# First half of the context finished inside the last group of heads, two unread matmuls in the first steps, copies ahead of the magnitudes

## What is computed

```python
q, k, v = x @ w_q.T, x @ w_k.T, x @ w_v.T           # 16 heads of 16
scores = where(mask, rope(q) @ rope(k).T * SCALE, -inf)
ctx = softmax(scores) @ v
x = layernorm(x + ctx @ w_o.T)
h = silu(x @ w_gate) * (x @ w_up)
h_sparse = the two largest magnitudes of every four
x = layernorm(x + h_sparse @ w_down)
```

## Time and profile before

| | us |
|---|---|
| median of 3 runs | 1748.93 (1747.69 to 1752.15) |
| profiled execution | 1751.17 |
| its span | 1749.4 |
| PE busy | 1486.2 (85%) |
| DVE busy | 1140.8 (65%) |
| ACT busy | 732.8 (42%) |
| POOL busy | 244.8 (14%) |
| granted clock of PE, mean | 0.914 of 2.4 GHz |

### The profile page before, as it was taken

One profiled execution on the slowest core, in us unless ns is written; L12 is line 12 of the kernel. 1 busy time (PEld: TensorE's weight loads), 2 busy tenths in 40 slices (PEclk: granted clock), 3 DMA queues, 4 the chain that ended last, 5 costly groups with the idle time before them and its releaser, 6 DMA issues.

```text
span 1749.4 us, 25732 instructions
## 1 busy us (share of the span) xinstructions
PE 1486.2 (85%) x9682; PEld 827.5 (47%) x9683; DVE 1140.8 (65%) x2275; ACT 732.8 (42%) x1232; POOL 244.8 (14%) x249
## 2 busy tenths in 40 slices
PE   4999999877989983589878988878998788988796
PEld 2666666653657873223343533253533254433355
DVE  5666666636421135678669779768779678688475
ACT  5444455512212220426744137843137752157530
POOL 3344444411410001000020000120000120000000
PEclk8999999978999977758999979998979998989999
DMA  2000001005105512222101022101022101221000
GB/s 111 13 25 25 24 26 33 24 13 180 36 24 148 157 38 105 42 37 43 31 16 34 1 43 55 37 19 31 6 38 56 43 19 25 37 34 34 31 1 25
DMA packets 137483, 75.21 MB, mean 43 GB/s; under 512 B 117648, under 2 KB 126352, under 8 KB 136592
## 3 DMA queue, kind: packets, MB, share of 16 engines
q1 hardware_dynamic: 136800, 72.02, 16.6%
q0 software_dynamic: 576, 1.77, 0.4%
HBM read 37.59 MB, written 9.06 MB: 27 GB/s over the span
## 4 chain that ended last, share of the span: by engine, by line
issue 58%; POOL 3%; DVE 0%; POOLq 0%; DVEq 0%
POOL xs_sb L1448 1%; POOL rs_sb L1442 1%; POOL ve_sb L1439 0%; POOL qks_sb L1462 0%; POOL v_sb L1460 0%; DVE bn_sb L1620 0%; POOL qks_sb L1452 0%; DVE x_sb_sb L1635 0%; POOLq L1159 0%; POOLq L66 0%; DVE mv_sb L1626 0%; DVEq L1159 0%; POOL v_sb L1459 0%; POOL qks_sb L1463 0%; DVE ident_h_sb L1808 0%
## 5 line engine op out<-in xcount | busy, mean ns | idle before, releaser
L1522 ACT ACTIVATE room_sb<-s_ps 128x1024 f32<-128x1024 f32 (+1 forms) x320 | 291.2, 941 | 173.7 <-PE s_ps L1965 169.8
L1686 DVE TENSOR_REDUCE mx_sb<-s_ps 128x1 f32<-128x512 f32 (+1 forms) x400 | 249.6, 650 | 73.1 <-PE s_ps L1941 46.8
L1938 PE MATMUL s_ps<-room_sb 48*128 48x512 f16 (+3 forms) x480 | 155.9, 362 | 30.2 <-DVE mx_sb L1681 17.1
L1985 PE MATMUL cm_ps<-room_sb,v_sb 128*32 128x512 f32 (+3 forms) x1536 | 171.3, 536 | 0.8 <-ACT room_sb L1528 0.8
L1965 PE MATMUL s_ps<-room_sb 51*128 51x128 f16 (+4 forms) x1152 | 154.1, 288 | 15.4 <-ACT room_sb L1522 10.6
L2080 PE MATMUL cm_ps<-w_fd_sb,room_sb 128*128 128x256 f32 x512 | 132.7, 408 | 13.3 <-DVE room_sb L1764 13.3
L1439 POOL TENSOR_TENSOR ve_sb<-mv_sb,eps_sb 128x4 f32<-128x4 f32 x24 | 5.0, 210 | 951.2 <-DVE mv_sb L1626 951.2
L396 DVE SCALAR_TENSOR_TENSOR x_sb_sb<-xp_sb,conv_w_sb,x_sb_sb 128x512 f32<-128x512 f32 x96 | 106.7, 1114 | 22.6 <-ACT x_sb_sb L319 20.5
L1938 PEld LDWEIGHTS s_ps<-room_sb 48*128 48x128 f16 x480 | 42.9, 96 | 165.3 <-DVE mx_sb L1686 84.4
L2080 PEld LDWEIGHTS cm_ps<-w_fd_sb,room_sb 128*128 128x128 f32 x512 | 98.3, 200 | 38.1 <-issue 14.1
L2067 PE MATMUL s_ps<-xbT_sb,w_fg_sb 128*128 128x512 f16 x384 | 103.3, 400 | 14.3 <-DVE ctok_sb L1734 12.7
(11 more groups left out here) (256 smaller groups left out, 2942.7 us busy)
## 6 DMA issues: line engine op xcount, KB each, us to landing
we_gu_sb<-we_gu SPq DMA_DIRECT2D x32, 352.0 KB
we_dn_sb<-we_dn SPq DMA_DIRECT2D x32, 176.0 KB
x_in_sb<-x SPq DMA_DIRECT2D x9, 512.0 KB, 3.6
rows<-x_sb_sb SPq DMA_DIRECT2D x8, 512.0 KB, 3.0
x_sb_sb<-rows SPq DMA_DIRECT2D x2, 2048.0 KB, 11.4
out<-x_sb_sb SPq DMA_DIRECT2D x8, 512.0 KB, 2.6
room_sb<-qks_sb SPq DMA_TRANSPOSE x88, 3.3
xp_sb<-w_in SPq DMA_DIRECT2D x1, 1024.0 KB, 5.6
```

The source lines that it names most:

```text
L1522: act.activation(weights[(g * NU + u) % SLOTS_P][:, 2 * pair:2 * pair + 2, 0:width(u) * P], W[s % 2][:, :, 0:width(u) * P], ACT.Exp, scale ...
L1686: dve.tensor_reduce(mx[:, pair, k % 2, slot:slot + 1], max_bank(g, m)[:, 0:count * P], AX.X, ALU.max, negate=True).then_inc(mx_ok, 1)
L1938: last = pe.matmul(bank[:, at * P:(at + plain) * P], query[head:head + NORM, i * P:(i + 1) * P], key[head:head + NORM, j * P:(j + plain) * ...
L1985: last = pe.matmul(O[32 * h:32 * h + 32, (i - half * GT) * P:(i - half * GT + count) * P], v[:, j, g * HG + h, :], weights[(g * NU + u) % ...
```

## The change

In the last group the first half of the context is transposed (steps 10 and 11), copied by DVE, projected (a tile in each of steps 13 to 16), added to x and normalised; its transposes for the hidden layer stand right behind the last weighted sums, ahead of the last sums' transposes, in the two halves of bank S[2]. Behind the heads only the second half of the context is transposed. Its projection stands on PE behind the first hidden chunk, ahead of the second tile's `qkv`. In each of the first eight steps of a sequence two unread 128x512 matmuls go ahead of the scores. In the rotation loop ACT copies the next tile ahead of the magnitude. The LayerNorms of the next x move to the end of the third group and the start of the fourth, "f" of a first half into the hidden layer of its own sequence (chunks 13 and 14), "f" of a second half to steps 3 and 6. `mv` and `rs` have two buffers each. The diff, cut to its core:

```diff
@@ -1251,12 +1251,12 @@
...
         for b in range(NB):
-            if b > 0:
-                ORDER += [("f", b - 1, 0), ("f", b - 1, 1)]
...
                 ORDER += [("x", b + 1, 0), ("x", b + 1, 1)]
-            ORDER += [("a", b, 0), ("a", b, 1)]
-        ORDER += [("f", NB - 1, 0), ("f", NB - 1, 1)]
+            if b > 0:
+                ORDER.append(("f", b - 1, 1))
+            ORDER += [("a", b, 0), ("a", b, 1), ("f", b, 0)]
+        ORDER.append(("f", NB - 1, 1))
...
@@ -1346,6 +1346,10 @@
...
             return S[0] if c == 0 and t % 2 else S[2]
+
+        def half_banks(s):
+
+            return (C, M) if s else (S[2][:, 0, :], S[2][:, 1, :])
...
@@ -1465,10 +1469,10 @@
...
                 kind, b, s = ORDER[k]
+                if (kind, s) == ("a", 0) and b + 1 < NB:
+                    x_low(b + 1, 0)
+                    x_low(b + 1, 1)
...
-                if (kind, s) == ("x", 1):
-                    x_low(b, 0)
-                    x_low(b, 1)
...
@@ -1537,13 +1541,13 @@
...
                             sums_copied(b, g, 0)
-                        if g == NHG - 1 and b + 1 < NB and s >= STEPS - 2:
-                            x_high(b + 1, s - STEPS + 2)
+                        if g == NHG - 1 and b + 1 < NB and s in (8, 9):
+                            x_high(b + 1, s - 8)
...
             def high_chunks(b, s):
-                wait(act, wo_mm, 2 * b + 2)
-                for f, bank in enumerate((C, M)):
+                wait(act, wo_mm, 3 * b + 2 + s)
+                for f, bank in enumerate(half_banks(s)):
...
@@ -1582,13 +1586,12 @@
...
                 heads(b)
-                wait(act, tc, 2 * b + 2)
-                act.activation(xbT[:, 1, :].rearrange("p (a c) -> p a c", a=2), S[1][:, :, :], ACT.Copy).then_inc(cTa_ok, 1)
+                high_chunks(b, 0)
+                wait(act, tc, 3 * b + 3)
+                act.activation(xbT[:, 1, 1, :], M, ACT.Copy).then_inc(cTa_ok, 1)
...
                     qkv_copied(c, 0)
-                high_chunks(b, 0)
-                if ahead:
...
@@ -1600,12 +1603,12 @@
...
                         part_copies(c, w + 1)
+                    if ahead and w + 2 < ST:
+                        qkv_copied(c, w + 2)
...
                         magnitude(b, w)
-                    if ahead and w + 2 < ST:
-                        qkv_copied(c, w + 2)
...
@@ -1620,10 +1623,28 @@
...
                 wait(dve, bn_ok, k + 1)
-                wait(dve, ln_ok, k)
+                wait(dve, ln_ok, k - 1)
...
                 for t in range(GT):
-                    last = dve.bn_aggr(mv[:, t, :], bn[:, t, :])
+                    last = dve.bn_aggr(mv[:, k % 2, t, :], bn[:, t, :])
+                last.then_inc(mv_ok, 1)
+
+            def first_stats(b):
+                k = LN["a", b, 0]
+                wait(dve, mv_ok, k)
+                for t in range(GT):
+                    if t % 2 == 0:
+                        wait(dve, wo_mm, 3 * b + t // 2 + 1)
+                        own = x_sb[:, b * ST + t:b * ST + t + 2, :]
+                        dve.tensor_tensor(own, S[2][:, t // 2, :].rearrange("p (t c) -> p t c", t=2), own, ALU.add).then_inc(xr_ok, 1)
+                        wait(dve, xr_ok, 3 * b + t // 2 + 1)
+                    last = dve.bn_stats(bn[:, t, :], x_tile(b, t))
+                last.then_inc(bn_ok, 1)
+                wait(dve, bn_ok, k + 1)
+                wait(dve, ln_ok, k - 1)
+                dve.sem_inc(passed, 1)
+                for t in range(GT):
+                    last = dve.bn_aggr(mv[:, k % 2, t, :], bn[:, t, :])
...
@@ -1795,11 +1815,22 @@
...
                                 maxima(b, of, low, high)
-                        if g == NHG - 1:
-                            if b > 0 and s in (2, 6):
-                                finish(b - 1, s // 4)
-                            if b + 1 < NB and s in (10, 14):
-                                layernorm("x", b + 1, s // 4 - 2)
+                        if b + 1 < NB and (g, s) == (NHG - 2, 16):
+                            stats("x", b + 1, 0)
+                        if b + 1 < NB and (g, s) == (NHG - 2, 18):
+                            stats("x", b + 1, 1)
+                            normal("x", b + 1, 0)
+                        if b + 1 < NB and (g, s) == (NHG - 1, 0):
+                            normal("x", b + 1, 1)
+                        if b > 0 and (g, s) == (NHG - 1, 3):
+                            wait(dve, f2_ok, 2 * b)
+                            stats("f", b - 1, 1)
+                        if b > 0 and (g, s) == (NHG - 1, 6):
+                            normal("f", b - 1, 1)
+                wait(dve, tc, 3 * b + 1)
+                dve.tensor_copy(xbT[:, 0, :, :], S[2][:, :, :]).then_inc(cTv_ok, 1)
+                first_stats(b)
+                normal("a", b, 0)
...
@@ -1830,17 +1861,13 @@
...
                 heads(b)
-                wait(dve, tc, 2 * b + 1)
-                dve.tensor_copy(xbT[:, 0, :].rearrange("p (a c) -> p a c", a=2), S[0][:, :, :]).then_inc(cTv_ok, 1)
-                attn_residual(b, 0)
-                wait(dve, xr_ok, 2 * b + 1)
-                stats("a", b, 0)
-                attn_residual(b, 1)
-                normal("a", b, 0)
...
+                wait(dve, tc, 3 * b + 2)
+                dve.tensor_copy(xbT[:, 1, 0, :], C).then_inc(cTv_ok, 1)
...
                     rotate(c, 0)
-                wait(dve, xr_ok, 2 * b + 2)
+                attn_residual(b)
+                wait(dve, xr_ok, 3 * b + 3)
...
@@ -1881,6 +1908,11 @@
...
                         maxima(c, 0, m + 2, m + 4)
+                        if w == 13:
+                            wait(dve, f2_ok, 2 * b + 1)
+                            stats("f", b, 0)
+                        if w == 14:
+                            normal("f", b, 0)
...
@@ -2011,6 +2044,9 @@
...
                                 for_maxima(b, of, low, high)
+                        if g == 0 and s < AHEAD:
+                            wait(pe, exp_ok, group(b, 0)(STEPS, LEAD + s))
+                            kept_busy(W[(s + 1) % 2][:, 0, :], 2)
...
@@ -2019,37 +2055,47 @@
...
                             sums_transposed(b, g, 0)
+                        if g == NHG - 1 and s in (10, 11):
+                            first_context_transposed(b, s - 10)
+                        if g == NHG - 1 and 13 <= s < 17:
+                            out_projection(b, S[2], 0, s - 13)
...
                 weighted(b, NHG - 1, NU - 1, 0)
+                half_transposed(b, 0)
...
+            def first_context_transposed(b, f):
+                wait(pe, cn_ok, group(b, NHG - 1)(2, LEAD + 1))
+                if f == 0:
+                    wait(pe, mx_ok, group(b, NHG)(2 * NX, LEAD))
+                for t in range(GT):
+                    last = pe.transpose(S[2][:, f, t * P:(t + 1) * P], ctok[:, t, f * P:(f + 1) * P], ident[:])
+                if f == KD - 1:
+                    last.then_inc(tc, 1)
+
...
-                wait(pe, cn_ok, 2 * NHG * b + LEAD + 2 * NHG)
-                for f in range(KD):
-                    for t in range(ST):
-                        last = pe.transpose(S[f][:, t // 4, (t % 4) * P:(t % 4 + 1) * P], ctok[:, t, f * P:(f + 1) * P], ident[:])
+                wait(pe, cn_ok, group(b, NHG - 1)(2, LEAD + 2))
+                for f, bank in enumerate((C, M)):
+                    for t in range(GT):
+                        last = pe.transpose(bank[:, t * P:(t + 1) * P], ctok[:, GT + t, f * P:(f + 1) * P], ident[:])
...
-            def out_projection(b):
-                wait(pe, cTv_ok, b + 1)
-                wait(pe, cTa_ok, b + 1)
-                for t in range(ST):
-                    bank = (CM, S[1])[t // 4]
-                    for k in range(KD):
-                        last = pe.matmul(bank[:, t % 4 // 2, (t % 2) * D:(t % 2 + 1) * D], xbT[:, k, t * P:(t + 1) * P],
-                                         w_o[:, k, :], start=(k == 0), stop=(k == KD - 1))
-                    if t % 4 == 3:
-                        last.then_inc(wo_mm, 1)
+            def out_projection(b, bank, s, t):
+                wait(pe, cTv_ok, 2 * b + s + 1)
+                if s == 1:
+                    wait(pe, cTa_ok, b + 1)
+                for k in range(KD):
+                    last = pe.matmul(bank[:, t // 2, (t % 2) * D:(t % 2 + 1) * D], xbT[:, s, k, t * P:(t + 1) * P],
+                                     w_o[:, k, :], start=(k == 0), stop=(k == KD - 1))
+                if t == GT - 1 or (s, t) == (0, 1):
+                    last.then_inc(wo_mm, 1)
...
                 wait(pe, ln_ok, LN["a", b, s] + 1)
-                if s == 1:
-                    wait(pe, xTv_ok, 2 * b + 1)
-                    wait(pe, xTa_ok, 4 * b + 2)
-                for f, bank in enumerate((C, M)):
+                for f, bank in enumerate(half_banks(s)):
...
@@ -2112,17 +2156,13 @@
...
-                heads(b)
...
                     pe.wait_ge(w_low, 4)
```

(10 more changed lines are left out.)

38 lines of the change are left out of this document (18 added, 20 removed).

## The result

The changed kernel takes 1722.41 us (1716.18 to 1725.0), the kernel before beside it 1748.31 (1747.51 to 1752.15): a ratio of 0.9844 (95% interval 0.982 to 0.9868), 25.9 us less, where 1719 was forecast. The profiled execution took 1723.16 us, its span 1721.3, against 1749.4 before, with a mean granted clock of 0.935 instead of 0.914.

A forecast was written before the change was run, and what follows sets the result against it. No engine bounds the whole kernel, so the attention phase was read in four stages. -15 - 14.1 - 5.5 + 4.3 = -30.3 gave 1720.9 us for the profiled execution, 1719 from the median (1705 to 1730, chance 0.55).

The forecast's parts named there:

- The unread matmuls: First group of heads: matmul pairs keep the clock up, so DVE work at half clock runs denser; -15 us (-20 to 0).
- The longer last group: Last group of heads: early transposes and projection exceed PE's spare time, so the last exponential ends 3.8 us later (2.5 to 5.5).
- The second rotation at T' + 21.4: Tail: second rotation starts 21.4 us after the new last exponential (T'), T+25.2 from the old (T); 8.1 us gained over three sequences.
- The last sequence: Sequence 3, without rotations: fourth hidden chunk at T+23.8 instead of 29.9 us behind the last exponential; 6 us gained.
- The copies: Rotation loop: ACT's copies ahead of the magnitude spare DVE up to 0.5 us in four chunks of three sequences; -5.5 (0 to -7.5).
- The moved LayerNorms: Next x's in third and fourth groups: no cost; first half's finishing one at hidden chunks 13 and 14: +4.3 us (0 to +10).
- Context half and LayerNorms together: Last group, tail and hidden layer: -14.1 us (-21 to -5) for the early context half, +4.3 for the moved LayerNorms.
- The cold pairs: Rival, first group: the clock falls all the same and unread matmuls run at half clock; +22 instead of -15, 1756 us; chance 0.09.
- The cold tail: Rival, new tail: the clock falls before tile 0's queries, hidden(0) costs 2.45 us more, four times; 1729 us; chance 0.13.
- Theory A: Whole kernel, the prediction's view: each part of the change earns its own gain in its own stage; no size given.
- C: Theory on the context half, the largest part by its lines: it earns little of its own; no size given.
- theory B: Whole kernel: much of the gain is the clock's, and what one part saves comes back as half clock elsewhere; no size given.

The follow-up runs named there:

- the pauses are filled: The changed kernel with more unread 128x512 matmuls in seven pauses of TensorE: 1710.95 us, ratio 0.9774.

## Why the prediction came out right, and where it did not

The forecast of 1719 lies 3 us under the median, and the sum of -30.3 stands against -28.0 in the span and -25.9 in the medians. The parts did less well than their sum.

**The unread matmuls, -15 (-20 to 0).** In its stage the term is right to a microsecond: the first groups are 15.8 us shorter, clock 1.00, DVE at 0.88. But the kernel got 8.7 to 10.9 of it. The step that failed is a silent one: the gain was taken from one stage of one trace as if the clock elsewhere, and in the other kernel, stayed as it was. It doesn't. Kept up in the heads of the kernel before, it fell in the old tail (5.3 us); and in the changed kernel without the pairs the half clock in the first groups is shorter than before, so that the pairs have 8.1 us to save there and not 15.8.

**The longer last group, 3.8 us (2.5 to 5.5).** 4.9 to 5.2. The mis-sized terms are the work, where a tile keeps the next scores waiting for 1.06 us and not 0.92, and the spare time: I counted 1.3 us of pauses as free for PE, but the steps in question became PE's, as taking out matmuls showed. The waits were sized well, 0.36 for 0.4.

**The second rotation at T' + 21.4.** 20.97 and 20.98 at full clock, 23.38 in sequence 0. The reckoning of the new tail holds step by step: in sequence 1 the first half is normalised at T + 2.58 (reckoned 2.5) and the projection done at T + 14.5 (15.0). The gain of 8.1 came out as 18.4 - 14.9 = 3.5: over three sequences the groups took 3.5 us more than I gave them, and the rotation was 2.0 late in sequence 0 and 0.4 early in the others.

**The last sequence, -6.** 9.3 less from T to the end, less the 5.2 of its group: 4.1. Hidden(0) runs at full clock there now, as I said, where the same six matmuls took 2.74 us before:

```profile
1630.06 1.47 PE L2111 MATMUL s_ps<-xbT_sb,w_fg_sb 128*128 128x512 f16 x6
```

**The copies, -5.5 (0 to -7.5).** 4.0 in the trace; nothing that the medians show as the kernel stands, 6.4 in the trace where the pauses are filled. There rotations follow one another at 4.44 us, the 4.45 that I named, against 4.96. Mechanism and size are right at a steady clock; as the kernel stands the gain is not shown.

**The moved LayerNorms, +4.3 (0 to +10) and 0.** 3.4 us between chunks 12 and 15. These rows show it:

```profile
1233.43 1.40 DVE L1623 BATCH_NORM_STATS2 bn_sb<-x_sb_sb 128x6 f32<-128x256 f32 x4
...
1235.75 0.23 PE L1971 MATMUL s_ps<-room_sb 48*128 48x128 f16 x1 [0.93 <-DVE mx_sb L1702]
...
1237.88 1.37 DVE L1656 TENSOR_SCALAR x_sb_sb<-x_sb_sb,mv_sb,rs_sb 128x256 f32<-128x256 f32 x4
```

PE waits 0.93 us for a maximum, not the 2 us that would have told against me. That the place is worth its price I did not see: in the heads the same LayerNorm makes the last group 5.7 and 6.4 us longer in sequences 1 and 2, falls included. The early x LayerNorms show no cost, as said: the third groups take 25.48 us in both kernels.

**Context half and LayerNorms together.** That -14.1 + 4.3 comes so close to the 9.9 us between the kernels with and without them is luck. The pieces in the trace give 3.5 + 4.1 - 3.4 = 4.2, which agrees with the 4 us at a steady clock; the rest of the 9.9 is, by that subtraction, half clock, above all in the old tail (5.4 us in sequences 1 and 2), which the prediction does not have.

**The rivals.** The cold pairs did not come, and the clock held behind the eighth step too. The cold tail came in one sequence of four and cost 2.4 us. That this is the price named (2.45) is chance: the rival put it in hidden(0), but the transposes and tile 0's queries and values paid it, and hidden(0)'s first six matmuls took 1.60 us instead of 1.46. The Trainium skill's page "TensorE: Matmul & The Clock Gate", section "Part 4: PE-mode transpose", says that the full clock does not engage for transposes. The rows L2083 disagree: the eight transposes, with the same pause of 0.81 us ahead of them, took 1.09 us in one sequence and 1.97 in another, so they ran at full clock in one of them.

Theory A is right inside each stage, and C for three sequences of four. Of theory B the runs show this much: with the pairs in, the clock fell in the old tail, and by the subtraction above the context half earned most of its 9.9 us by taking that tail away. A return of half clock in the changed kernel itself did not show. The parts as I put them: pairs 11, copies with pairs 6 (1738.49 to 1732.35), context half and LayerNorms 10, of which some 6 are clock.
